# Row maxima of the attention scores: five of sixteen units per span taken as a + relu(b - a)

## What is computed

```python
h = _modulate(_layernorm(x), shift_msa, scale_msa)
qkv = h @ W_qkv + b_qkv
scores = jnp.einsum('blhd,bmhd->bhlm', q * scale, k)
attn = jax.nn.softmax(scores, axis=-1)          # 1024 keys for each query
o = jnp.einsum('bhlm,bmhd->blhd', attn, v).reshape(b, l, c)
x = x + gate_msa * (o @ W_proj + b_proj)
```

## Time and profile before

| what | value |
|---|---|
| median of 3 runs | 1539.19 us (1531.56 to 1539.38) |
| profiled execution | 1537.64 us, span 1535.9 us |
| TensorE busy | 1398.4 us, 91% |
| VectorE busy | 1094.9 us, 71% |
| ScalarE busy | 837.1 us, 55% |
| GpSimd busy | 631.3 us, 41% |
| granted TensorE clock, mean | 0.947 |
| layer 0: opening, then steps | 101 to 134 us, then 134 to 494 us |
| layer 1: opening, then steps | 741 to 773 us, then 773 to 1131 us |

### The profile page before, as it was taken

How to read it: one execution, slowest core, us unless ns; L and a number is a source line. 1 busy time by engine, 2 the same in 40 slices (tenths; PEclk the granted TensorE clock), 3 DMA queues, 4 the chain that set the end, 5 groups by cost and what they waited for, 6 DMA issues and landing times. The chain is left out here.

```text
span 1535.9 us, 27833 instructions
## 1 busy us (share of the span) xinstructions
PE 1398.4 (91%) x9997; PEld 869.7 (57%) x9997; DVE 1094.9 (71%) x1847; ACT 837.1 (55%) x1575; POOL 631.3 (41%) x870
## 2 busy tenths in 40 slices
PE   5978999999998989989889999999994699999994
PEld 3754333333333778967633333333353699999994
DVE  3546899989992646766579999999647365666653
ACT  3635777877886431155477787787831233333331
POOL 2146533553000435534489887796016112121121
PEclk8986999999999999999689999999997799999997
DMA  7577534543001188427732321130059477676763
GB/s 187 163 175 119 131 89 100 137 107 72 3 3 33 51 244 267 162 70 232 173 57 50 49 49 32 23 47 3 3 199 326 139 231 201 209 232 186 237 198 77
DMA packets 93839, 194.66 MB, mean 127 GB/s; under 512 B 35734, under 2 KB 63448, under 8 KB 90716
## 3 DMA queue, kind: packets, MB, share of 16 engines
q1 hardware_dynamic: 61802, 117.93, 24.3%
q0 software_dynamic: 31600, 73.00, 21.2%
q10 hardware_dynamic: 306, 2.00, 0.6%
HBM read 127.27 MB, written 66.68 MB: 126 GB/s over the span
## 5 line engine op out<-in xcount | busy, mean ns | idle before, releaser
L1120 ACT ACTIVATE att_probs<-att_scores 128x512 f32<-128x512 f32 x1002 | 541.6, 604 | 141.0 <-PE att_scores L1271 132.7
L1135 DVE TENSOR_REDUCE att_neg_max<-att_for_max 128x1 f32<-128x1024 f32 x472 | 569.8, 1222 | 49.7 <-PE att_for_max L1228 40.5
L1283 PE MATMUL att_out<-att_probs,V 128*32 128x256 f32 (+1 forms) x3232 | 308.8, 454 | 2.9 <-ACT att_OZ L1097 1.9
L1228 PE MATMUL att_for_max<-att_KS,att_QS 54*128 54x512 f32 x640 | 243.7, 455 | 6.7 <-DVE att_neg_max L1135 6.7
L1271 PE MATMUL att_scores<-att_QS,att_KS 56*128 56x512 f32 x618 | 226.9, 453 | 0.9 <-DMA att_QS<-att_neg_max_rows 0.9
L2177 ACT ACTIVATE experts_gelu<-experts_proj,experts_b 128x256 f32<-128x256 f32 x171 | 81.1, 474 | 208.4 <-PE experts_proj L2246 187.8
L2246 PE MATMUL experts_proj<-experts_x_parts,w_parts 128*128 128x256 f32 (+1 forms) x1197 | 174.0, 286 | 1.2 <-DVE experts_x_parts L1984 1.2
L1271 PEld LDWEIGHTS att_scores<-att_QS,att_KS 56*128 56x128 f32 x618 | 95.0, 185 | 132.5 <-ACT att_probs L1120 116.6
L2135 POOL DMA_INDIRECT sums_of_experts<-experts_y,experts_rows x38 | 61.1, 1608 | 260.1 <-DVE experts_y L2020 254.3
L2246 PEld LDWEIGHTS experts_proj<-experts_x_parts,w_parts 128*128 128x128 f32 (+1 forms) x1197 | 157.8, 191 | 5.2 <-issue 3.6
L1271 PE MATMUL att_scores<-QS,KS 56*128 56x512 f32 x384 | 147.9, 463 | 12.9 <-DMA QS<-att_neg_max_rows 10.3
(11 more groups left out here) (297 smaller groups left out, 2204.4 us busy)
## 6 DMA issues: line engine op xcount, KB each, us to landing
w_parts<-w_parts SPq DMA_DIRECT2D x19, 2304.0 KB
qk_halves<-qkv_qk_parts SPq DMA_DIRECT2D x40, 288.0 KB
w_parts<-w_parts SPq DMA_DIRECT2D x4, 2592.0 KB
slot_rows<-mlp_blank_rows SPq DMA_DIRECT2D x2, 5145.0 KB
att_QS<-qk_halves POOLq DMA_DIRECT2D x120, 72.0 KB, 4.5
att_KS<-qk_halves POOLq DMA_DIRECT2D x60, 144.0 KB, 4.9
w_parts<-w_parts SPq DMA_DIRECT2D x19, 432.0 KB
experts_rows<-slot_rows SPq DMA_DIRECT2D x19, 294.0 KB, 9.8
```

The costliest lines, as they stand in the source:

```text
L1120: nc.scalar.activation(PR[st % 2][:, j, :], score_bank(st, n), ACT.Exp, scale=SCALE).then_inc(exp_done, 1)
L1135: nc.vector.tensor_reduce(negm[half][:, c:c + 1], psM[ring % 2][:].rearrange("p a n -> p (a n)"), AX_X, ALU.max, negate=True).then_inc(rin ...
L1228: last = nc.tensor.matmul(psM[ring % 2][:, keys, :], QS[s][rows, half, p, t * P:(t + 1) * P], KS[s][rows, p, keys * BLK:(keys + 1) * BLK], ...
L1283: last = nc.tensor.matmul(psO[32 * j:32 * j + 32, n0:n1], T.V[:, g, k, 32 * j:32 * j + 32], PR[st % 2][:, j, n0:n1], start=(k == 0 and n0 ...
```

## The change

Five units of a span's sixteen take the form of the opening: the first unit of steps 0, 2, 5, 6 and 7, wherever units are still due. Such a step has on TensorE `difference` in two parts and `first_half` instead of two `max_half`, which is one matmul more; on ScalarE a Relu of 128 x 512 behind exponential 1; on VectorE `half_max` instead of `reduce`. The negated keys are made anew for each next group, half of them at the end of ScalarE's step 3 and half at the end of its step 4 of the group's first span. The Relu results get buffers of their own, and with that ScalarE's wait for the end of the opening goes. One buffer instead of two holds split weights in layer 0. SyncE's store of the first turned maxima comes ahead of the four loads of modulation rows. TensorE gets six filler matmuls of 128 x 512 before its wait at the end of the opening.

```diff
@@ -823,10 +823,16 @@
+def folded(st):
+
+    return bool(units_of(st)) and st % KT in (0, 2, 5, 6, 7)
...
@@ -868,8 +875,7 @@
-            S = Splitter(nc, T, pieces, sb("w_f32", [P, FF], F32), [sb(f"w_parts{n}", [P, 2, FF], F32R) for n in range(2)],
-                         sem)
+            S = Splitter(nc, T, pieces, sb("w_f32", [P, FF], F32), [sb("w_parts", [P, 2, FF], F32R)], sem)
...
-        gains = [PR[1][:, n, :] for n in range(2)]
-        PLAIN, HEAD_SLOTS = 2, 3
+        gains = [sb(f"gain{n}", [P, BLK], F32) for n in range(2)]
+        PLAIN, HEAD_SLOTS, MINUS_AT = 2, 3, 3
...
+        halved = [q for q in range(PLAIN, UNITS + AHEAD)] + [units_of(st)[0] for st in range(STEPS) if folded(st)]
+        halved = {q: f for f, q in enumerate(halved)}
+        by_place = list(halved)
...
@@ -968,10 +974,11 @@
                 sp.wait_ge(rows_out, NA)
                 sp.dma_start(T.ada_scr, arow[:, 0:6 * C]).then_inc(row_stored, 16)
                 sp.wait_ge(row_stored, 16)
+            store_max(0)
+            if early:
                 for dst, part in spread_rows:
                     src = T.ada_scr[:, part * C:(part + 1) * C].rearrange("(o b) c -> o b c", o=1)
                     sp.dma_start(dst, src.broadcast_to([P, B, C])).then_inc(wide_in, 16)
-            store_max(0)
...
@@ -1097,18 +1104,20 @@
+            def gain(q, other):
+                f = halved[q]
+                act.wait_ge(diff_ready, f + 1)
+                if f >= 2:
+                    act.wait_ge(ring_read, item[by_place[f - 2]] + 1)
+                nc.scalar.activation(gains[f % 2][:], other, ACT.Relu).then_inc(gain_ready, 1)
...
-            act.wait_ge(ring_read, HEAD_ITEMS)
...
@@ -1121,6 +1130,15 @@
                                          ).then_inc(exp_done, 1)
                     if n == 0 and (span := span_behind(st, COPY_LAG)) is not None:
                         finish(span)
+                    if n == 1 and folded(st):
+                        q = units_of(st)[0]
+                        gain(q, psM[item[q] % 2][:, 1, :])
+                g = st // (HALVES * KT) + 1
+                p = st % (HALVES * KT) - MINUS_AT
+                if 0 <= p < PAIRS and g < GROUPS:
+                    act.wait_ge(loaded[g % SLOTS], ((g - (0 if g % SLOTS else SLOTS)) // SLOTS + 1) * LOADS)
+                    nc.scalar.activation(minus[:, p, :], KS[g % SLOTS][:, p, 0:BLK].bitcast(F32), ACT.Copy, scale=-1.0
+                                         ).then_inc(minus_ready, 1)
...
@@ -1174,14 +1192,15 @@
-            def head_max(q):
+            def half_max(q):
...
-                here = head_banks(ring)[0]
+                here = head_banks(ring)[0] if q < UNITS + AHEAD else psM[ring % 2][:, 0, :]
+                f = halved[q]
                 dve.wait_ge(ring_ready, ring + 1)
-                dve.wait_ge(gain_ready, q - PLAIN + 1)
-                nc.vector.tensor_tensor_reduce(out=here, in0=here, in1=gains[q % 2], scale=-1.0, scalar=LARGEST,
+                dve.wait_ge(gain_ready, f + 1)
+                nc.vector.tensor_tensor_reduce(out=here, in0=here, in1=gains[f % 2][:], scale=-1.0, scalar=LARGEST,
                                                op0=ALU.add, op1=ALU.min, accum_out=negm[half][:, c:c + 1]
                                                ).then_inc(ring_read, 1)
...
                 for q in units_of(st):
-                    reduce(q)
+                    if q in halved:
+                        half_max(q)
+                    else:
+                        reduce(q)
...
@@ -1286,6 +1308,29 @@
+            def difference(q, part):
...
+                if part == 0:
+                    if q % (HALVES * UNITS) == 0 and g:
+                        pe.wait_ge(loaded[s], ((g - (0 if s else SLOTS)) // SLOTS + 1) * LOADS)
+                    ring_free()
+                    nc.tensor.matmul(psM[ring % 2][:, 1, :], queries, KS[s][rows, p, BLK:2 * BLK], start=True, stop=False)
+                else:
+                    pe.wait_ge(minus_ready, 1 + PAIRS * g)
+                    nc.tensor.matmul(psM[ring % 2][:, 1, :], queries, minus[rows, p, :], start=False, stop=True
+                                     ).then_inc(diff_ready, 1)
+
+            def first_half(q):
...
+                nc.tensor.matmul(psM[ring % 2][:, 0, :], QS[g % SLOTS][rows, half, p, t * P:(t + 1) * P],
+                                 KS[g % SLOTS][rows, p, 0:BLK], start=True, stop=True).then_inc(ring_ready, 1)
+                ring += 1
...
@@ -1333,16 +1378,22 @@
+            keep_busy(nc, T, psS[1][:], 6)
             pe.wait_ge(ring_read, HEAD_ITEMS)
             for st in range(STEPS):
...
                 score(st, 0)
-                if units:
+                if folded(st):
+                    difference(units[0], 0)
+                elif units:
                     max_half(units[0], 0)
                 score(st, 1)
-                if units:
+                if folded(st):
+                    difference(units[0], 1)
+                    first_half(units[0])
+                elif units:
                     max_half(units[0], 1)
```

More of the change, by code:

```diff
@@ L823, in span_behind @@
     return span - 1 if rest == 0 and span > 0 else None
+def folded(st):
+    return bool(units_of(st)) and st % KT in (0, 2, 5, 6, 7)
 def ring_counts():
-    n, maxima, turned, divided = 0, {}, {}, {}
+    n, maxima, turned, divided, item = 0, {}, {}, {}, {}
     for q in range(UNITS + AHEAD):
+        item[q] = n
         n += 1
@@ L847, in ring_counts @@
     divided[SPANS - 1] = n + 1
-    return maxima, turned, divided
+    return maxima, turned, divided, item
 def attention_stage(nc, T, l, W, pieces):
@@ L912, in attention_stage @@
         minus = sb("minus_keys", [P, PAIRS, BLK], F32R)
-        gains = [PR[1][:, n, :] for n in range(2)]
-        PLAIN, HEAD_SLOTS = 2, 3
+        gains = [sb(f"gain{n}", [P, BLK], F32) for n in range(2)]
+        PLAIN, HEAD_SLOTS, MINUS_AT = 2, 3, 3
         HEAD_ITEMS = UNITS + AHEAD + 1
-        def head_item(q):
-            return q + (q > UNITS + 1)
         def head_banks(n):
@@ L929, in attention_stage @@
         ROWS_AT, COLUMNS_AT, MOD_AT = (1, 3, 5), 8, 13
-        maxima, turned, divided = ring_counts()
+        maxima, turned, divided, item = ring_counts()
+        halved = [q for q in range(PLAIN, UNITS + AHEAD)] + [units_of(st)[0] for st in range(STEPS) if folded(st)]
+        halved = {q: f for f, q in enumerate(halved)}
+        by_place = list(halved)
         def score_bank(st, n):
@@ L1099, in _ @@
             nc.scalar.activation(minus[:], T.KS0[:, :, 0:BLK].bitcast(F32), ACT.Copy, scale=-1.0).then_inc(minus_ready, 1)
-            for q in range(PLAIN, UNITS + AHEAD):
[L1101 to L1105, removed]
+            def gain(q, other):
[4 more added lines that the diff above has]
+                nc.scalar.activation(gains[f % 2][:], other, ACT.Relu).then_inc(gain_ready, 1)
+            for q in range(PLAIN, UNITS + AHEAD):
+                gain(q, head_banks(item[q])[1])
                 if early and q == ROWS_AT[-1]:
@@ L1192, in _ @@
                 else:
-                    head_max(q)
+                    half_max(q)
                 if q == UNITS + 1:
@@ L1287, in weigh @@
                     last.then_inc(pv_done, 1)
+            def difference(q, part):
+                g, half, i, p, t = unit_at(q)
+                s = g % SLOTS
+                rows = slice(i * LANES, i * LANES + ROWS)
+                queries = QS[s][rows, half, p, t * P:(t + 1) * P]
+                if part == 0:
[8 more added lines that the diff above has]
+            def first_half(q):
+                nonlocal ring
+                g, half, i, p, t = unit_at(q)
+                rows = slice(i * LANES, i * LANES + ROWS)
+                nc.tensor.matmul(psM[ring % 2][:, 0, :], QS[g % SLOTS][rows, half, p, t * P:(t + 1) * P],
+                                 KS[g % SLOTS][rows, p, 0:BLK], start=True, stop=True).then_inc(ring_ready, 1)
+                ring += 1
             def head_free():
```

## The result

The changed kernel takes 1606.34 us (median of 4 runs, 1602.12 to 1608.13) against 1536.49 for the kernel before: ratio 1.0458, 95% interval 1.0422 to 1.0494. It is 4.6% slower. Its profiled execution took 1605.05 us with a span of 1603.2.

The account below looks back on a forecast made before the run. TensorE and VectorE both looked full, with the ring of two pairs binding in places. 1537.6 + 39.4 + 35.6 - 2.2 - 2.0 = 1608.4 us profiled, forecast 1609 us; range 1540 to 1662 us, chance 0.8.

Parts of the forecast that it names:

- The folded unit: Units folded in steps 0, 2, 5, 6 and 7 make a span 2.65 us longer, 38.0 us a layer.
- The chain: In a folded step, exponential 0 at 0.59 us after score 0, Relu 1.57, maximum 2.32, place usable by TensorE at 3.13.
- second place: The second unit's place is free 4.21 us after score 0, for 3.69 and 3.21 before in steps 5 and 7.
- "+0.23 each": In steps 6 and 0 TensorE's third matmul stands alone on its rows and adds 0.23 us each.
- Negated keys: ScalarE's copy in step 4 delays step 5 by about 0.2 us (0 to 0.6), seven times: 1.4 us a layer.
- Layer 1: VectorE's wait for the Relu hides stretched small operations, 0.47 us in each of eight spans; the layer gets +35.6 us.
- give-back: In layer 1, 3.8 us regained over eight spans because VectorE will be waiting for the Relu.
- The start: Storing before the row loads in layer 0 brings the first score 2.2 us sooner (0 to 3).
- The fillers' "0 (at most 0.3)": Six filler matmuls, about 2.8 us at half clock, fit TensorE's wait before the first score and cost 0, at most 0.3.
- gain of 1 us a layer: The filler matmuls may bring the full clock back sooner: -1 us a layer (0 to -5).
- Rival 1, the clock: Longer waits in steps 5 and 6 make TensorE's clock fall in half of 28 spans: +35, 1644 us, chance 0.12.
- Rivals 2 and 3: Only lone matmuls cost, 1566 us, chance 0.12; VectorE's relief makes a span 0.97 us shorter, 1506 us, chance 0.14.

## Why the prediction was right, step by step

*The folded unit.* The chain held to 0.02 us at each of its stations (0.60, 1.57, 2.31, 3.13; second place at 4.20), because each came from a row of a like operation. By pairs, a fold and the step that waits for it: 5 with 6, +0.46 + 0.28 = 0.74 (0.75 in the prediction); 7 with 0, +0.52 + 0.70 = 1.22 (1.23); 2 with 3, +0.23 + 0.43 = 0.66 (0.67). A span grew by 2.62 for 2.65. Moving the Relu by one place in ScalarE's order took back 1.40 of it (1.42 by the same steps). The late Relu is thus shown as the cause of more than half of the loss, the lone matmuls with 0.90 as that of a third. The 0.32 that are left are not shown by a run of their own; with the earlier Relu, step 7 to step 0 still takes 3.70 us for 3.21, of which the lone matmul accounts for 0.23.

*One term was right by its surroundings.* "+0.23 each" for steps 6 and 0 is true only behind a wait. Alone the two cost 0.79. The prediction did not say why the chain should not bind in step 0; by the rows of the two traces the reason is ScalarE's lead during the wait (the Relu 1.04 us behind the difference, not 1.42).

*Negated keys.* 0.20 in each span with copies, 0 to 0.6 having been the bounds: spans alternate between 24.55 and 24.75.

*Layer 1.* Its undisturbed spans are 24.55 and 24.75 too, as forecast, but not for the reason given. That VectorE's wait hides the stretched small operations is shown by the run with only step 5 folded: one of them takes 0.42 to 0.81 us in eleven spans of layer 1, and all but one of these spans are 22.43 or 22.63 as in layer 0. In the changed kernel there was little to hide: they take 0.17 to 0.20 us in all but two spans. The give-back was 5.1 us and not 3.8, since eleven spans had been longer, not eight.

*The forecast's 3 us too many.* 1608.4 for the profiled execution, 1605.05 measured. Layer 0 of the kernel before held two disturbed spans (22.89 and 24.99, 4.0 us above 21.93), which the sum carried over as if they would come again; after, one span of layer 0 was 0.92 longer. In layer 1 a span of 27.13 added 2.6, against the larger give-back. Ahead of layer 1's steps there is luck. From its first score to its first reciprocal it took 44.5 us for 38.7, 5.8 more where the forecast's terms give 2.75 (2.65 + 0.90 + 0.2 - 1); 17.1 us of it lie at the low clock, 12.0 before. From the last reciprocal of layer 0 to that score it took 291.5 for 297.3, 5.8 less where the forecast has none. The two cancel.

*The start.* The first score was to come 2.2 us sooner. In the profiles it came from 5.09 to 2.97 behind the stores, which looks like this number, but that is luck, and the parts are others: the order alone gives 3.7, outside the 0 to 3 that the prediction allowed, and the fillers take 1.6 back. The fillers' "0 (at most 0.3)" failed too, since they were set against a wait of 2.6 us that the new order had already shortened to 1.2. Their gain of 1 us a layer is not shown either: in layer 1 the clock was full from the fillers' end for 3.4 us and then fell. The stretch behind it:

```profile
798.60:801.60 3.00, 2.15 (x10) 1.09 (x10) 0.73 (x3) 2.45 (x6) 2.82 (x5) 1.00 0.50 115
802.00:818.00 16.00, 16.00 (x80) 5.52 (x78) 8.72 (x9) 8.49 (x17) 15.94 (x17) 0.50 0.59 102
```

*Rival 1, the clock.* Its frequency was not reached: two falls in 26 spans. Its price, 2.5 us for 6.8 us at low clock, was met (27.13 - 24.55 = 2.58), but that span held more than a fall. These rows lie ahead of it, with the fall at 1095.1:

```profile
1089.62 2.25 POOL L1026 TENSOR_TENSOR att_router_products<-att_router_rows,w_proj 128x1152 f32<-128x1152 f32 x1
1090.23 1.67 DVE L1174 CAST att_inverse_parts<-att_inverse 128x16 fp32r<-128x16 f32 x1
...
1092.87 0.28 PE L1264 MATMUL att_for_max<-ident,att_neg_max 128*16 128x128 f32 x1 [0.90 <-DVE att_neg_max L1203]
```

One of the small operations behind the reciprocal took 1.67 us for 0.17 and ended with GpSimd's instruction, VectorE was late, and TensorE waited 0.90 us. The other runs show the same: outside the one with the later Relu, the whole spans of the thirteen kernels hold 14 falls, each 4 to 6 us behind the reciprocal, and in 13 of these spans a small operation took 0.74 to 2.64 us. The span without one is that of the changed kernel's fall in layer 0 (3.4 us at low clock, the span 0.92 longer). The six falls of 6.8 us came with spans 2.5 to 4.5 us longer. What part of that is the clock's is not shown.

The clock was nearer than its chance of 0.12 suggests. With the Relu half a microsecond later still, it is low for half of the time. The Trainium skill, "TensorE: Matmul & The Clock Gate", section "Why this matters for your kernels", blames one long idle gap for such drops; that late-Relu run speaks against it as the only cause, with 16 falls in the spans of layer 0 and no wait of a maxima matmul over 0.9 us there.

*Rivals 2 and 3.* The lone matmul alone costs 0.90 a span and not 1.15: 1558 us in its one run, 1541 for the kernel before beside it. The relief is worth 0.64 at most. Its point of decision, a second place free before 3.21 in step 7, was never reached: 3.70 with the earlier Relu.

## What to carry to other kernels

When work moves from a full engine to one with room, ask where in the receiver's order it will stand and who waits for its result; a share of free time does not say when the free time is. Before such a move, halve the work of the full engine with nothing put in its place: if that run gains less than the new work costs elsewhere (here 0.64 us a span against 0.90), expect the move not to pay. And where TensorE waits often and briefly, half a microsecond more in the chain can cost far more than half a microsecond, since the clock may go with it.

## What the runs showed of the hardware

- TensorE's granted clock fell without a long wait. TensorE was busy for 282 of 288 us in the spans of layer 0 before and for 304 of 321 after, with one fall each. In the run with the later Relu, where it was busy for 16.24 of 20 us at the full clock and no maxima matmul waited for over 0.9 us, the clock fell 16 times in 437 us.
- In the changed kernel six filler matmuls in the wait ahead of the first score lifted the clock, but it fell again 3.4 us after their end, for 6.8 us in layer 0 and 17.1 in layer 1, while TensorE's first steps themselves waited (2.15 us busy of the 3.0 from 798.6 on).
- VectorE's small operations of 0.17 us took over 0.3 us, up to 2.64, in 125 cases of the fourteen profiles, and 124 of these ended within 0.12 us behind the end of a GpSimd instruction on elements; the row of 1.67 us above is one. Others ran beside such an instruction and took 0.17. Why some are held up and others not is not shown. Whether a span gets longer by it depends on the room behind them: 22.5 for 21.93 in layer 1 before, nothing with only step 5 folded, and 22.35 for 21.29 in every second span with VectorE's work taken away, where one takes 1.2 us.
